# Reordering the end of a linear-attention stage, and splitting its weights one block earlier

## The reference, cut to what matters

```python
xn = _layernorm(x)                         # 2048 x 512
q, k, v = heads(xn @ q_w.T + q_b), ...     # 16 heads of 32
qp = elu(q) + 1; kp = elu(k) + 1
kv = einsum('bhsd,bhse->bhde', kp, v)      # 32 x 32 for each head
z  = einsum('bhsd,bhd->bhs', qp, kp.sum(axis=2))[..., None]
attn = einsum('bhsd,bhde->bhse', qp, kv) / (z + 1e-6)
out = attn @ o_w.T + o_b
```

## Time and profile before

| | us |
|---|---|
| median of three runs (lowest, highest) | 1543.32 (1541.33, 1543.69) |
| profiled execution, its own time | 1543.52 |
| span of its trace, first to last instruction | 1541.8 |
| PE busy | 1471.3 (95%) |
| DVE busy | 1029.9 (67%) |
| ACT busy | 755.4 (49%) |
| POOL busy | 461.0 (30%) |
| `stage_attend0` in the trace | about 427.7 to 506 |

### The profile page before, as it was taken

One profiled execution on the slowest core, in us unless ns is written; L12 is line 12 of the kernel. 1 busy time (PEld: TensorE's weight loads), 2 busy tenths in 40 slices (PEclk: granted clock), 3 DMA queues, 4 the chain that ended last, 5 costly groups with the idle time before them and its releaser, 6 DMA issues. The chain is left out here.

```text
span 1541.8 us, 23547 instructions
## 1 busy us (share of the span) xinstructions
PE 1471.3 (95%) x6981; PEld 1062.9 (69%) x6981; DVE 1029.9 (67%) x2939; ACT 755.4 (49%) x1282; POOL 461.0 (30%) x691
## 2 busy tenths in 40 slices
PE   6999999999998999999989999999999998898998
PEld 4778788888776788788855555555555545687776
DVE  5453666666657656887767886665668974578592
ACT  5623556556564544433325555555555562235561
POOL 0000677777610112323221212221212213054062
PEclk9999999999999999999969999999999999999999
DMA  5001222211110334366797405314134017744021
GB/s 185 1 1 70 95 76 75 112 75 75 55 48 7 130 110 125 121 193 197 193 236 282 110 19 120 74 55 120 35 92 120 13 62 208 247 171 155 22 89 14
DMA packets 107124, 161.53 MB, mean 105 GB/s; under 512 B 12352, under 2 KB 63696, under 8 KB 100624
## 3 DMA queue, kind: packets, MB, share of 16 engines
q1 hardware_dynamic: 101868, 153.64, 32.6%
q10 hardware_dynamic: 4516, 5.38, 1.0%
q0 software_dynamic: 640, 1.31, 0.4%
HBM read 117.44 MB, written 42.87 MB: 104 GB/s over the span
## 5 line engine op out<-in xcount | busy, mean ns | idle before, releaser
L2138 ACT ACTIVATE l_pt<-banks 128x1024 f32<-128x1024 f32 (+3 forms) x288 | 218.6, 811 | 140.2 <-PE banks L2013 138.3
L2210 DVE CUSTOM_DVE_ANT_0 stage<-banks,l_edges 128x384 f32<-128x384 f32 (+3 forms) x384 | 201.7, 542 | 73.1 <-issue 71.8
L2050 PE MATMUL banks<-l_pt,l_v 128*64 128x512 f32 (+3 forms) x1152 | 222.0, 507 | 2.0 <-POOL l_pt L2108 2.0
L718 POOL TENSOR_TENSOR ex_hl<-ex_h,ex_hh 128x512 fp32r<-128x512 f32 x128 | 165.6, 1301 | 81.1 <-ACT ex_hh L686 81.0
L2107 POOL TENSOR_TENSOR l_turn<-l_before 128x2 f32<-128x2 f32 x192 | 38.6, 201 | 385.0 <-ACT l_pt L2138 375.4
L751 DVE SCALAR_TENSOR_TENSOR ex_rw<-banks,ex_wb 128x512 f32<-128x512 f32 x128 | 88.3, 691 | 78.9 <-PE banks L75 78.8
L2213 DVE TENSOR_REDUCE l_mx<-banks 128x1 f32<-128x384 f32 (+1 forms) x208 | 113.1, 544 | 39.9 <-PE banks L1991 39.2
L2050 PEld LDWEIGHTS banks<-l_pt,l_v 128*64 128x64 f32 x1152 | 69.3, 138 | 91.4 <-issue 68.2
L686 ACT ACTIVATE ex_hh<-ex_h 128x512 fp32r<-128x512 f32 x128 | 80.9, 632 | 103.6 <-DVE ex_h L759 103.4
L73 PE MATMUL banks<-ex_xlh,ex_wh 128*128 128x512 f32 x256 | 101.7, 397 | 2.0 <-DVE ex_rw L751 2.0
L74 PE MATMUL banks<-ex_xll,ex_wh 128*128 128x512 f32 x256 | 99.8, 390 | 0.0
(11 more groups left out here) (454 smaller groups left out, 3496.9 us busy)
## 6 DMA issues: line engine op xcount, KB each, us to landing
ex_wb<-gates_by_expert SPq DMA_DIRECT2D x16, 1024.0 KB, 4.6
l_v<-layer_v SPq DMA_DIRECT2D x8, 1024.0 KB, 16.9
layer_qk<-qkv_yh SPq DMA_DIRECT2D x30, 256.0 KB, 3.2
layer_qk<-qkv_yl SPq DMA_DIRECT2D x30, 256.0 KB, 3.6
layer_v<-qkv_vs SPq DMA_DIRECT2D x15, 512.0 KB, 5.0
ex_ws<-ew_in SPq DMA_DIRECT2D x16, 384.0 KB, 5.0
l_q<-layer_qk SPq DMA_DIRECT2D x12, 512.0 KB, 7.7
l_k<-layer_qk SPq DMA_DIRECT2D x12, 512.0 KB, 13.3
```

What stands on the lines that cost most here:

```text
L718: pool.tensor_tensor(hl[:, k % RING, :], h[:, k % RING, :], raw(hh[:, k % RING, :]), ALU.subtract).then_inc(hl_done, 1)
L2050: last = pe.matmul(bank[h * 2 * HD:(h + 1) * 2 * HD, (qa - b * BT) * P:(qz + 1 - b * BT) * P], v[par][:, kt, h, :], pt[:, step_part(b, j), ...
L2138: act.activation(pt[:, step_part(b, j), :, 0:width], G.banks[:, 2 * slot:2 * slot + 2, 0:width], ACT.Exp, scale=scale).then_inc(p_done, 1)
L2210: dve.tensor_tensor_reduce(cutoff[:, n % 4, 0:width], G.ps[5 + n % MB][:, 0:width], masked, 1.0, NEG, ALU.add, ALU.max, mx[:, h, m, c:c + ...
```

## The change

Three edits, all in `stage_attend0`. The weight pieces are split four behind block 0 and four behind block 1, and none behind block 2. The tail of PE takes folded(2) and folded(3) ahead of the last two spreads of block 2, puts the last sums behind all of these, and places all four last spreads between the second and the third of three shared parts. DVE takes weighed(1,3) ahead of feature(3,3), takes folded(0) and folded(1) ahead of weighed(2,0) and weighed(2,1), and moves the last inverses behind folded(2), folded(3), weighed(2,2) and weighed(2,3).

```diff
@@ stage_attend0
-        cuts = [0, 3, 6, 8]
+        cuts = [0, 4, 8, 8]
@@ tensor
             weights.ready(pe, 2)
             shared_part(0, "swg")
-            sums(NB - 1)
+            folded(2)
+            folded(3)
             spread(NB - 2, 2)
             spread(NB - 2, 3)
-            folded(2)
-            folded(3)
+            sums(NB - 1)
             shared_part(0, "sw1")
             shared_part(1, "swg")
-            spread(NB - 1, 0)
-            spread(NB - 1, 1)
+            for g in range(NC):
+                spread(NB - 1, g)
             shared_part(1, "sw1")
-            spread(NB - 1, 2)
-            spread(NB - 1, 3)
@@ vector
             for b in range(NB - 1):
                 for g in range(NC):
+                    if b == NB - 2 and g == NC - 1:
+                        weighed(b - 1, g)
                     feature(b + 1, g)
-                    if b >= 1:
+                    if b >= 1 and not (b == NB - 2 and g == NC - 1):
                         weighed(b - 1, g)
                     if g == 0:
                         inverses(b)
                 weights.low(dve, cuts[b], cuts[b + 1])
+            folded(0)
+            folded(1)
             weighed(NB - 2, 0)
             weighed(NB - 2, 1)
-            folded(0)
-            folded(1)
-            inverses(NB - 1)
             folded(2)
             folded(3)
             weighed(NB - 2, 2)
             weighed(NB - 2, 3)
+            inverses(NB - 1)
             for g in range(NC):
                 weighed(NB - 1, g)
```

## The result

The changed kernel took 1534.55 us (median of five runs, 1534.13 to 1535.13) against 1543.21 for the kernel before (five runs, 1541.33 to 1543.69). The ratio is 0.9947 with an interval of 0.9931 to 0.9963. The forecast was 1536.1 in a range of 1534.0 to 1538.6. The kernel became faster by 8.7 us where 7.2 were forecast. The interval of the ratio stands for 5.7 to 10.6 us, so this comparison alone doesn't tell 8.7 from 7.2.

A forecast was written before the change was run, and what follows sets the result against it. PE, busy 95% of the span, sets the time, so only its tail stalls and slow clock pay: 7.5 - 0.2 - 0.1 = 7.2 us off 1543.52 gives 1536.3, median 1536.1, range 1534.0 to 1538.6.

The forecast's parts named there:

- The four stalls: PE's tail: 1.56 us before spread(2,1), 0.70 before the first shared part, 1.77 before shared_part(1, swg), 1.41 at stage's end; all go.
- the 1.56 us wait: PE's tail, before spread(2,1): PE waits for weighed(1,3), which stood behind feature(3,3) on DVE; forecast gone.
- The warm spacing: PE's tail: 0.233 us per matmul by the trace, not the skill's 216 ns, which would save 1.2 us more.
- The loop: Blocks 0 and 1: one more weight piece behind each makes spread(0,3) some 0.2 us late; bounds 0 and 0.7.
- The tightest place: PE's tail: spread(3,0) due at 494.5, its inverses done at 494.4; cover 0.1 us, stall taken 0.1, bounds 0 and 1.
- The rival that ACT and DVE set the tail: Tail: stalls turn into others of equal length, time 1543.3 us; chance 0.05, shared with inverses wholly uncovered.
- The stage's sum: Touched stage: 7.5 us gained, less 0.2 in the loop and 0.1 at the inverses, gives 7.2 us.
- the rest should move forward as a whole: Next stages: ACT and DVE enter together with PE and the first 48 matmuls wait for nothing.
- 1.5 us to either side: Whole program: allowance for clock dips elsewhere, from the 2.4 us by which three runs of before differ.
- after the three stalls: PE's tail: some eight matmuls ran at the lower clock, 0.427 us each, costing 1.55 us.
- its staying: Rival for the tail's clock: the slow stretch stays or turns up elsewhere, 1.55 us less saved, 1537.7; chance 0.09.
- the term of 1.55 us: PE's tail: the saving counted for the slow clock's going, part of the 7.6 us from the stalls.

The follow-up runs named there:

- experiment three: The changed kernel with weighed(1,3) behind feature(3,3) again on DVE: 1536.75 us, ratio 0.9964.
- four: The changed kernel with spreads (3,2) and (3,3) behind shared_part(1, sw1) again on PE: 1536.78 us, ratio 0.9959.
- five: The changed kernel with the last sums (PE) and inverses (DVE) ahead of folded(2) and folded(3) again: 1539.95 us, ratio 0.9990.
- two: The changed kernel with the old weight cuts [0, 3, 6, 8], so the tail's new order alone: 1538.28 us, ratio 0.9977.
- Experiment seven: The changed kernel with 12 redundant matmuls, computing shared_part(1, swg) a second time ahead of it: 1540.49 us, ratio 0.9983.
- Experiment ten: The changed kernel with the fourth weight piece split inside block 1 instead of behind block 0: 1534.93 us, ratio 0.9941.
- Experiment six: The changed kernel with the last four spreads ahead of shared_part(1, swg), one shared part as cover: 1538.90 us, ratio 0.9976.
- experiment nine: The changed kernel once more, unaltered, beside the kernel before on one chip: 1536.21 us against 1543.60, ratio 0.9953.
- experiments one: The kernel before with weight cuts [0, 4, 8, 8] alone: 1540.72 us against 1541.81, ratio 0.9986.
- eight: The changed kernel with weighed(1,3) behind feature(3,3), and sums and inverses ahead of folded(2) and folded(3): 1540.10 us, ratio 0.9986.

## Why the prediction was right, and where it was off

**The four stalls.** All four went, as forecast. Put back one at a time, three of them cost 1.82 (experiment three), 1.10 (four) and 2.0 (five, without its slow stretch of about 1.55 us); for the weight pieces' stall 1.95 came back (two), since in the new tail PE reaches that place earlier. None hides another except the weight pieces' one, behind the 1.56 us wait: 0.7 us alone, 1.95 once that is gone. So the edit of the weight pieces looks poor alone only since the wait ahead of it is still there.

**The warm spacing.** The tail took 18.66 us against 18.6 forecast (498.7 - 480.08). Experiment seven measured the spacing as 2.78/12 = 0.232 us, so going by the trace was right. The 216 ns of the Trainium skill, "TensorE: Matmul & The Clock Gate", section "Back-to-back issue gap", don't hold for these matmuls. The section calls them the gap of an isolated matmul and gives about 131 ns for a stream of weight loads and matmuls of 512 columns; these traces, with a weight load for every matmul, don't agree with that either.

**The loop.** I took 0.2 us for a late spread(0,3); the trace has 0.24. weighed(0,1) ends at 464.70 + 0.68 = 465.38 and the spread starts at 465.43, where its place after the matmul at 465.07 would have been 465.30; the restart adds the rest. Experiment ten removed it.

**The tightest place.** I reckoned 0.1 us of cover for the last inverses and took 0.1 us of stall. Measured, they end at 493.08 + 0.75 = 493.83, the last matmul before the spreads starts at 493.77, and spread(3,0) starts 0.24 behind it at 494.01: cover just under 0.2 us, stall none, though the weight load of the spread waited 0.15 us for them. Experiment six shows that the cover is real: with one shared part instead of two, PE stood still for 2.51 us.

**PE as the bound.** The rival that ACT and DVE set the tail is refuted by experiment seven: with that rival 12 more matmuls would have cost less than 0.8 us, and they cost 2.78.

**The stage's sum** was 7.2 us (7.5 - 0.2 - 0.1) and came out as 7.19. Its terms came out as 7.43, 0.24 and nothing, so part of the agreement is that small errors cancel. In the total the forecast was 1.5 us too slow. The step that was mis-sized is the last of the walk, that "the rest should move forward as a whole": in the profiled pair the rest also became 1.17 us shorter, and what lies before the stage 0.74, with the same instructions. I had left that to chance and given it 1.5 us to either side.

**Where the pair's other 1.9 us lie.** The traces place most of it. Of the 0.74 us ahead of the stage, 0.66 arise in the first 16 us of the program. There matmuls first follow each other at 0.43 us, the spacing of the lower clock in the tail; the windows show a granted clock of 1.00 there all the same, so this is read from the spacing. It falls to 0.23 from 14.40 us on in the changed kernel's execution, but in the other's not before 15.65. The rows where it changes, changed kernel first, then the kernel before:

```profile
14.01 0.55 PE L74 MATMUL banks<-kv_wkl,xTh 128*128 128x512 f32 x1
14.40 0.39 PE L75 MATMUL banks<-kv_wkh,xTl 128*128 128x512 f32 x1
...
15.22 0.63 PE L74 MATMUL banks<-kv_wkl,xTh 128*128 128x512 f32 x1
15.65 0.51 PE L75 MATMUL banks<-kv_wkh,xTl 128*128 128x512 f32 x1
```

Behind the stage, 0.6 us arise at one place, the end of the output stage, where PE waited 2.83 us instead of 3.41:

```profile
624.20 0.27 PE L1560 MATMUL banks<-ident,score 128*16 128x128 f32 x1 [2.83 <-PEq L1056]
...
632.78 0.27 PE L1560 MATMUL banks<-ident,score 128*16 128x128 f32 x1 [3.41 <-PEq L1056]
```

The same wait takes 3.53 us in the changed kernel's other profiled execution (experiment nine), and from 2.62 to 3.56 in all traces, so it is scatter from one execution to the next and not a gain of the change. Behind PE's last matmul stand 8.0 us before and 7.6 after. The rest is small differences of both signs. Nor does the pair's mean clock explain the 1.9 us: it is 0.981 in both. The changed kernel lost the slow stretch in the tail and had a longer one elsewhere (the window from 1311 to 1321 stands at 0.66; the same work before, from 1320 to 1330, at 0.83).

**The clock over many runs.** Each run is listed with its mean granted clock. Over 66 runs of the kernel before on the experiments' chips, the time falls as the mean clock rises, with a correlation of -0.83, and a line through all the runs of the experiments (one level for each kernel) falls by 1.0 us for each 0.001 of mean clock. On one chip the kernel before took 1534.55 us at 0.987 and 1548.35 at 0.976. So most of the spread of the totals goes with the mean clock. Slow stretches do come and go: between 620 and 640 us the traces of both kernels have one (a window of ten at 0.83), and that of experiment six has none (1.00). With the line taken off, the changed kernel of experiment nine is 6.2 us (5.0 to 7.3) faster than the kernel before at the same mean clock. That interval covers the stage's 7.2 and also 7.2 - 1.55 = 5.65, what is left if the line takes the going of the tail's slow stretch off too; it doesn't cover 8.7. So the rival of experiment nine, 8.7 us again at the same mean clock, is not borne out, and the medians differ by 7.4. That the first comparison's other 1.5 us are scatter is what the runs favour. They don't show it: of its runs only the two profiled ones can be followed in time, its five runs of the changed kernel were all at 0.981 or 0.982, and of its runs of the kernel before only the profiled one's clock (0.981) is known.

**The slow stretch in the tail.** The prediction said that it stood "after the three stalls" and counted 1.55 us for its going, with 0.09 for its staying. It did go: in the changed kernel, and in eight of the ten experiments with the new tail or most of it, the windows from 480 to 510 stand at 1.00. It went with one stall, the third, PE's wait for the folded remainders: the four traces with that wait of 1.77 to 1.78 us (before, experiments one, five and eight) all have the slow stretch behind it, and the nine without it have none in the tail. So "after the three stalls" was too wide: the third, put back alone, was enough. Why that one and not the others is open (each of these programs has one trace), and with it the reason for the term of 1.55 us, which came true without having been worked out. Neither length nor place tells it apart: the stall of experiment six began 64.4 us behind the stage's first matmul, that of experiment five 64.3, and it was longer (2.51 us), yet the clock stayed at 1.00, as it did behind 1.93 us (two).

## What to carry to other kernels

When one engine has stalls in a row, work out the timeline of all engines with the durations from the trace and move every late item at once: here one edit alone gave 0.7 us and was worth 1.95 once the stall ahead of it was gone. A long instruction chain on another engine (here 5.3 us of inverses) wants work of the bounding engine beside it that is at least as long, and what others wait for should stand ahead of it. And measure a gain of half a per cent by the stage in the trace as well as by the total: here the stage took 71.21 and 71.17 us in two executions, while the totals of one kernel spread over more than ten.

## What the runs showed of the hardware that was not expected

The clock can fall behind a short stall, but the length does not decide it: 1.78 us was enough in experiment five (window 490 to 500 at 0.83), and 2.51 us in experiment six left it at 1.00. In experiment five the ten matmuls from 494.79 to 498.67 took 3.88 us instead of 10 x 0.233 = 2.33, so the stretch cost 1.55 us. It is a price that a stall may bring beyond its own length, here nearly as large as the stall itself.
